# Audio tower on one core: gathers laid out by token quarter, head and slot, an 8-column weight matrix, and a third dense head

## The reference, cut to what matters

```python
kv_scores, indices = _pk(x, Wq_pk, pk_keys)     # per token and head: the 16 best of 4096 rows, with softmax weights
k = jnp.einsum('bnhk,bnhkd->bnhd', kv_scores, keys_table[ind])
v = jnp.einsum('bnhk,bnhkd->bnhd', kv_scores, values_table[ind])
sim = jnp.einsum('bihd,bjhd->bhij', q, k)       # then causal softmax, times v, times Wo
```

## Time and profile before

| | |
|---|---|
| median of 3 runs | 6525.63 us (6495.56 to 6534.32) |
| span of the profiled execution, first to last instruction | 4037.6 us |
| what lies around the span (median less span) | 2488.0 us |
| instructions in the trace | 71484 |
| mean granted clock of TensorE | 0.933 |
| PE, DVE, ACT, POOL busy | 88%, 72%, 68%, 73% of the span |
| indirect DMAs, size | 3072, 201.5 MB |

### The profile page before, as it was taken

How to read it: one execution, slowest core, us unless ns; L and a number is a source line. 1 busy time by engine, 2 the same in 40 slices (tenths; PEclk the granted TensorE clock), 3 DMA queues, 4 the chain that set the end, 5 groups by cost and what they waited for, 6 DMA issues and landing times.

```text
span 4037.6 us, 71484 instructions
## 1 busy us (share of the span) xinstructions
PE 3556.1 (88%) x21240; PEld 2640.5 (65%) x21240; DVE 2916.6 (72%) x13918; ACT 2746.8 (68%) x7870; POOL 2942.1 (73%) x3079
## 2 busy tenths in 40 slices
PE   9789999999989888889888889888889888889677
PEld 6367666667666666667666666666667666667556
DVE  3577778887777777777777777777777777777661
ACT  4467777777767677767677767677767677767444
POOL 0477777777777777777777777777777777777776
PEclk9699999999999999999999999999999999999788
DMA  3112222222222222222222222222222222222211
GB/s 115 30 51 53 54 54 54 53 54 55 54 53 54 54 53 55 54 54 54 55 53 54 54 54 54 54 53 54 54 54 54 54 53 54 54 54 54 53 53 50
DMA packets 108453, 220.17 MB, mean 55 GB/s; under 512 B 55768, under 2 KB 56192, under 8 KB 107552
## 3 DMA queue, kind: packets, MB, share of 16 engines
q0 software_dynamic: 98304, 201.52, 19.0%
q1 hardware_dynamic: 9760, 14.08, 1.1%
HBM read 214.36 MB, written 1.05 MB: 53 GB/s over the span
## 4 chain that ended last, share of the span: by engine, by line
POOL 37%; PE 21%; DVE 15%; issue 15%; ACT 11%; DMA 1%; DVEq 0%; SPq 0%; POOLq 0%; ACTq 0%
POOL got L755 37%; PE bank L1062 5%; ACT diag L1307 3%; PE bank L843 2%; DVE pick L1736 2%; DVE dist L1740 2%; PE bank L1039 2%; PE bank L826 1%; ACT L1093 1%; PE bank L1017 1%; PE bank L829 1%; ACT d_exp L1286 1%; DMA got<-in_table,rows 1%; DVE d_w L1774 1%; DVE rowf L1670 1%
## 5 line engine op out<-in xcount | busy, mean ns | idle before, releaser
L755 POOL DMA_INDIRECT got<-in_table,rows x3072 | 2940.9, 957 | 1085.5 <-issue 925.3
L1307 ACT ACTIVATE diag<-cst,weight 128x128 f32<-128x128 f32 x3072 | 944.7, 393 | 1.0 <-PE bank L1062 0.4
L1062 PE MATMUL bank<-diag,got 128*128 128x128 f32 x6144 | 803.0, 294 | 17.1 <-DMA got<-in_table,rows 9.3
L1062 PEld LDWEIGHTS bank<-diag,got 128*128 128x128 f32 x6144 | 770.3, 207 | 41.5 <-issue 19.5
L1039 PE MATMUL bank<-d_w,tab 128*128 128x128 f32 x4096 | 646.3, 283 | 0.5 <-DVE d_w L1774 0.5
L1774 DVE SCALAR_TENSOR_TENSOR d_w<-bank,d_exp 128x256 f32<-128x256 f32 x1024 | 420.7, 421 | 259.8 <-ACT d_exp L1286 109.3
L1039 PEld LDWEIGHTS bank<-d_w,tab 128*128 128x128 f32 x4096 | 553.8, 196 | 13.2 <-issue 0.8
L1286 ACT ACTIVATE d_exp<-bank 128x256 f32<-128x256 f32 x1024 | 378.2, 376 | 189.8 <-PE bank L1019 188.9
L1017 PE MATMUL bank<-d_top,sel 128*128 128x512 bf16 x1024 | 400.6, 391 | 116.8 <-DVE d_w L1774 116.5
L843 PE MATMUL bank<-h,conv_w 128*128 128x512 f32 (+2 forms) x1024 | 337.7, 478 | 9.3 <-DVE h L1430 7.1
L1017 PEld LDWEIGHTS bank<-d_top,sel 128*128 128x128 bf16 x1024 | 115.5, 113 | 267.0 <-DVE d_w L1774 167.8
(11 more groups left out here) (307 smaller groups left out, 6400.6 us busy)
## 6 DMA issues: line engine op xcount, KB each, us to landing
got<-in_table,rows POOLq DMA_INDIRECT x3072, 2.5
tab<-in_table SPq DMA_DIRECT2D x2, 2048.0 KB, 16.7
got<-in_pairs SPq DMA_DIRECT2D x1, 2048.0 KB, 8.8
wave<-in_x SPq DMA_DIRECT2D x32, 50.0 KB
cst<-in_consts SPq DMA_DIRECT2D x1, 1059.0 KB, 6.9
mlp<-in_mw SPq DMA_DIRECT2D x1, 1024.0 KB, 9.4
out_h<-res_o SPq DMA_DIRECT2D x32, 32.0 KB
conv_w<-in_w SPq DMA_DIRECT2D x1, 512.0 KB, 4.0
```

The source lines that it names most:

```text
L755: pool.indirect_dma_start(got[:, g, k, :], None, table, bass.IndirectOffsetOnAxis(ap=rows[:, h * TOPK + k:h * TOPK + k + 1], axis=0)).then ...
L1062: last = mm(kvt_ps, got[:, j % NGB, k, :], diag[:, j % NDG, k, :], start=k == 0, stop=k == TOPK - 1)
L1307: last = a(diag[:, (b * NG + h) % NDG, k, :], const("ident"), ACT.Copy, scale=weight[:, b % 2, h, k:k + 1])
```

## The change

- Four heads are gathered in pairs, head 4 alone, and heads 5, 6 and 7 are dense. Row numbers and weights are turned by VectorE in 32 x 32 blocks, so that a gather of 128 rows is 4 tokens (one of each quarter) times 2 heads times 16 slots; head 4 is gathered as two halves of the quarter. There are 5 groups of 16 gathers per batch in place of 6.
- A gathered block is multiplied by a matrix of 8 columns (`spread_w`): each column holds the 16 weights of one token and head. VectorE makes it in one instruction per group. The diagonal matrices and the ScalarE work on them are gone, and so is the adding up of 16 products.
- Dense head 5 gets units of its own: 16 "one" units of two chunks each between the 32 "two" units of heads 6 and 7. In a "one" unit ScalarE makes a penalty out of the list distance, TensorE adds it to the scores by a product with `unlisted`, and ScalarE's exponential writes the weights directly; VectorE has no part in it. `UNITS` is 48.
- `rows` gets two buffers, `kvt` one per gathered head, `got` has three in place of four. The dense stage, the sums and the heads become stages of their own in a new table of due times.

```diff
-DENSE = (6, 7)
+DENSE = (5, 6, 7)
...
-UNITS = CHUNKS
+SPLIT = [part for w in range(CHUNKS // 2) for part in (("two", 2 * w), ("two", 2 * w + 1), ("one", 2 * w))]
+UNITS = len(SPLIT)
...
-NGB = 4
+NGB = 3
+SLOTS = 8
...
-        rows = sb("rows", [P, HEADS * TOPK], U32)
...
+        rows = sb("rows", [P, 2, NG * TOPK], U32)
...
+                        if n >= NGB and k % QUARTER == 0:
+                            pool.wait_ge(s_summed, (n - NGB) * (TOPK // QUARTER) + k // QUARTER + 1)
+                        pool.indirect_dma_start(got[:, n % NGB, k, :], None, table,
...
+                    if SOFT[u]:
+                        last = mm(ps[:, 1, at], sel[:, c, :], d_top[:, 1, of, :].rearrange("k i t -> k (i t)"), start=first, stop=end)
...
+                        for i, (c, at) in enumerate(lists):
+                            for k, part in enumerate((d_top[:, 0, of, :], d_mid[:, of, :], d_low[:, of, :])):
+                                mm(pair_bank[u % 2][:, at], sel[:, c, :], part.rearrange("k i t -> k (i t)"), start=i == k == 0, stop=False)
+                        mm(pair_bank[u % 2][:, 0:2 * P], unlisted[:, :], d_pen[:, SOFT_UP_TO[u] % 2, :], start=False, stop=True).then_inc(s_d_out, 1)
...
-                    mm(acc_bank[:, 0:ND * P], const("neg_iota", 0, 1).broadcast_to([P, P]), cst[:, 0:ND * P], start=True, stop=False)
...
+                    last = mm(kvt_ps[:, k * SLOTS:(k + 1) * SLOTS], got[:, n % NGB, k, :], spread_w[:, n % NGB, k, :], start=True, stop=True)
...
-                        last = mm(kvt_ps, got[:, j % NGB, k, :], diag[:, j % NDG, k, :], start=k == 0, stop=k == TOPK - 1)
...
+                        a(d_pen[:, SOFT_UP_TO[u] % 2, :], pair_bank[u % 2][:, 2 * P:4 * P], ACT.Relu, bias=eps[:, 3:4]).then_inc(s_d_pen, 1)
...
+                        a(d_w[:, u % 2, :, :].rearrange("p k t -> p (k t)"), scores, ACT.Exp).then_inc(s_d_soft, 1)
...
-                        last = a(diag[:, (b * NG + h) % NDG, k, :], const("ident"), ACT.Copy, scale=weight[:, b % 2, h, k:k + 1])
...
-                if not isinstance(b, int) or b > 0:
-                    for h in range(first, end):
-                        vec.wait_ge(s_got[((b - 1) * NG + h) % NGB], (((b - 1) * NG + h) // NGB + 1) * 16 * TOPK)
...
+                tt(rows[:, b % 2, a:z], turned[:, a:z], const("row_base", a, z), ALU.add).then_inc(s_rows, 1)
...
+                tt(spread_w[:, n % NGB, :, :].rearrange("p j (q o) -> p j q o", q=4), share, slots, ALU.mult).then_inc(s_spread, 1)
```

More of the change, by code:

```diff
@@ L42 @@
 CHUNKS = NKEY * NKEY // P
-UNITS = CHUNKS
+SPLIT = [part for w in range(CHUNKS // 2) for part in (("two", 2 * w), ("two", 2 * w + 1), ("one", 2 * w))]
+UNITS = len(SPLIT)
+SOFT = [kind == "one" for kind, _ in SPLIT]
+SOFT_UP_TO = [sum(SOFT[:u + 1]) for u in range(UNITS)]
+HARD_UP_TO = [u + 1 - n for u, n in enumerate(SOFT_UP_TO)]
 LORA = 64
@@ L656, in in_turn @@
-        def in_turn(count, late, unit, first, last):
-            def both(prev, cur):
-                if prev is not None:
-                    for u in range(count - late, count):
-                        yield from unit(prev, u)
-                    yield from last(prev)
-                if cur is not None:
-                    yield from first(cur)
-                    for u in range(count - late):
-                        yield from unit(cur, u)
-            return both
+        HOPS = (names(T_HOPS), names(MIX_HOPS), names(ROUTE_HOPS), names(SECOND_HOPS), names(DENSE_HOPS),
+                names([x for g in range(NG) for x in sum_hops(g)]), names([x for p in range(HEADS) for x in head_hops(p)]))
@@ L669, in nothing, with each, program @@
+        def each(count, unit):
+            def program(b):
+                for u in range(count):
+                    yield from unit(b, u)
+            return program
         def nothing(*_):
             return iter(())
-        qpk = diag[0:32, 0, 0:8, :].rearrange("p k d -> p (k d)")
-        pkk = diag[0:32, 0, 8:16, :].rearrange("p k d -> p (k d)")
+        qpk = got[0:32, 2, 0:8, :].rearrange("p k d -> p (k d)")
+        pkk = got[0:32, 2, 8:16, :].rearrange("p k d -> p (k d)")
         LOADS_0 = [(cst[:, 0:CONST_FIRST], consts[:, 0:CONST_FIRST]), (chan[:, :], cvec)]
@@ L1041, in table_sum @@
-                last.then_inc(s_d_sum, 1)
+                listed(b, u)
+                if u == 0 and b > 0:
+                    pe.wait_ge(s_kvd, b)
+                kind, c = SPLIT[u]
+                for i in range(2):
+                    of, chunk = (1 + i, c) if kind == "two" else (0, c + i)
+                    last = mm(acc_bank[:, of * P:(of + 1) * P], tab[:, of, chunk, :], d_w[:, u % 2, i, :],
+                              start=u == i == 0, stop=u == UNITS - 1 and i == 1)
+                last.then_inc(s_d_sum, 1)
@@ L1083, in head @@
                 mm(y_ps, prob_t[:, :], vw[:, :], start=True, stop=True).then_inc(s_y, 1)
-            pipeline(pe, tokenizer, mixer, nothing, dense, nothing, in_turn(HEADS, SCORES_LATE, head, nothing, nothing))
+            pipeline(pe, tokenizer, mixer, nothing, nothing, dense, each(NG, group), each(HEADS, head))
         @block.scalar
@@ L1326, in head @@
                 a(prob_t[:, :], prob_ps, ACT.Copy).then_inc(s_prob_t, 1)
-            pipeline(act, tokenizer, mixer, second, dense, in_turn(NG, SUMS_LATE, weighted, nothing, nothing),
-                     in_turn(HEADS, SCORES_LATE, head, nothing, nothing))
+            pipeline(act, tokenizer, mixer, route, second, dense, each(NG, group), each(HEADS, head))
         @block.vector
@@ L1675, in choose @@
                     yield f"l{k}"
[L1676 removed]
+                    for i in range(of):
                         for r0 in (0, 4):
@@ L1802, in head @@
                 stt(res_o[:, :] if p == HEADS - 1 else res[:, b % 2, :], y_ps, erec[:, :], res[:, b % 2, :], ALU.mult, ALU.add).then_inc(s_added, 1)
[L1804 to L1809 removed]
+            pipeline(vec, tokenizer, mixer, route, second, dense, each(NG, group), each(HEADS, head))
 _OUT = (BATCH, C, D)
```

467 lines of the change are left out of this document (244 added, 223 removed), and 158 rows, old and new, of tables (AT, ENDS_AT).

## The result

The changed kernel took **7348.09 us** (median of 4, 7327.61 to 7358.18) beside 6529.98 us of the kernel before (6495.56 to 6536.48): 1.124 times as long, 95% interval 1.1195 to 1.1287. Slower was right; 7348 lies outside the range of 6240 to 7060.

A forecast was written before the change was run, and what follows sets the result against it. GpSimd's gathers bound the kernel, TensorE close behind; then TensorE: 105.9 + 14.1 + 8.5 - 2.0 = 126.5 us per batch against 119, +240 us, ends +15, so 6525.6 + 255 = 6780 us (+3.9%), range 6240 to 7060.

The forecast's parts named there:

- The starting point, 119 us: Present batch period, set by GpSimd's gathers: 96 gathers at 1.24 us each take 119 us.
- TensorE's added work, +14.1: On TensorE, 16 new "one" units less 16 fewer gathered blocks and smaller items: net +14.1 us per batch (12.2 to 19.1).
- the fall behind L826: Half clock on TensorE after its wait at L826, said to go with that wait: -2.0 us per batch.
- The clock, +8.5: Five gathered groups of 8-column products per batch each cost TensorE one 3.4 us stretch at half clock: 8.5 us.
- the upper bound of 17: Clock price per batch if each group costs two half-clock stretches, or the next group itself runs at 1.2 GHz.
- Idle time, taken as cancelled: TensorE's other 8 idle us per batch, of which some stay, taken to cancel against modelled tails of 0.16 us per gap.
- The wait for landed gathers: VectorE's wait at L1569 before writing new row numbers, 4.8 us per batch, said to go because `rows` has two buffers.
- The ends, +15: The end of the run gets some 15 us longer, since the last batch's 48 units stand alone.
- I take this remainder as unchanged: The 2488 us between the profiled span and the median time, assumed to stay the same after the change.
- both upper prices: Rival, chance 0.12: clock and bf16 products both at their upper price, 140 us per batch, 7210 us.
- TensorE packs perfectly: Rival, chance 0.25: TensorE has no idle time and no group costs clock, period 111 us, 6285 us, faster.
- no clock loss: Rival, chance 0.15: groups on TensorE cost no clock, otherwise as forecast, 118 us per batch, 6510 us, same time.

The follow-up runs named there:

- changed, windows: Changed kernel with block k multiplied by weight columns of blocks k to 15, 68 on average, sums kept: 4185.49 us without stalls, 7188.80 with.

## Why the prediction was wrong

A period is here the time from the first group of batch 8 to that of batch 24, by 16, in traces without stalls:

| us per batch | period | TensorE busy | idle |
|---|---|---|---|
| before | 121.0 | 106.9 | 14.1 |
| changed | 147.6 | 142.5 | 5.1 |
| changed, 128 columns | 125.9 | 120.3 | 5.6 |
| changed, windows | 123.5 | 117.9 | 5.6 |
| before, 8 columns | 133.8 | 131.1 | 2.7 |

- **The starting point, 119 us: too low by 2.** The period of before is 121.0. The prediction took 1.24 us for a gather; their starts are 1.25 apart in the median but 1.263 in the mean, and 96 x 1.263 = 121.2. Its own figure of 1.264 had said so.
- **TensorE's added work, +14.1: right.** At the usual clock (128 columns) it is 120.3 - 106.9 = +13.4, beside 14.1 - 2.0 = 12.1, since the fall behind L826 is in it (half clock for 423 us instead of 519, 1.5 us per batch). Of its parts, the 16 blocks kept their pace: at full clock a group takes 3.5 to 3.7 us to the next instruction with 8, 68 or 128 columns alike, so the columns don't set it. The bf16 products of 128 columns start 0.055 us apart, the lower bound; I had taken 0.07. The Trainium skill ("TensorE: Matmul & The Clock Gate", section on the back-to-back issue gap) has about 81 ns; this trace doesn't agree.
- **The clock, +8.5: the step that failed.** It measured 147.6 - 125.9 = **+21.7**. The step was "if each group costs one stretch of 3.4 us at half clock", with "the units between the groups are dense enough to bring the clock back". The mechanism was right, the size wasn't: a group brings 11.6 us of half clock, of which 2.6 were there anyway (420 us in 160 groups), so 9.0 more, half of it lost, 4.5 x 5 = 22 us. Nor did the units between the groups bring the clock back in time: 81 of the 160 groups ran at half clock from end to end. Even the upper bound of 17 was too low, because it counted a fall or a slow group; here one group makes the clock fall, and the next one, which runs inside the fall, holds it down. The earlier trace rows gave the price of a slow group, and I didn't ask what the slow group does to the clock behind it.
- **Idle time, taken as cancelled: wrong by 5.** 5.1 to 5.6 us are left beside work that fills TensorE. The stop at L826 is gone as said: its successor L743 has 12.8 us of idle time ahead of it in the whole run without stalls, where L826 had 129.8.
- **The wait for landed gathers** is gone, VectorE's 97 us are 925.11 / 1200 x 125.9 = 97.1, ScalarE's 67 are 72. GpSimd stands waiting for L999, as said, but without stalls only 214 us in all; it waits far longer (1396 us) for VectorE's row numbers at L1527, and the prediction did not have this wait.
- **The ends, +15: wrong in sign.** Before 4035 - 32 x 121.0 = 163 us, after 4862 - 32 x 147.6 = 139: -24.
- **The sum.** Period +26.7 instead of +7.5 (the clock 13.2 more, idle time 5.1, starting point and busy time the rest), ends -24 instead of +15: +830 by these, +820 measured, +255 predicted.
- **"I take this remainder as unchanged": the second step that failed.** The 2488 us are not around the span, they are stalls inside it, and the profile of before came from an execution that had none. As a number it came out unchanged, 7348 - 4859 = 2489. That is chance rather than a rule: for the version with windows it is 7189 - 4185 = 3004, for the kernel before with 8 columns 6743 - 4484 = 2259, and spacing the gathers takes nearly all of it away. So the share of time that the stalls hold was the largest thing there was to gain, and the prediction had put it out of sight. The sign was there to be questioned: a page whose span is 38% below every time beside it describes another sort of execution.

Of the rivals, "both upper prices" (7210 us, 0.12) was nearest. Of its two causes the clock was right, and larger than it had it (21.7 us against 17); the bf16 products came out at their lower price, not the upper. "TensorE packs perfectly" fell with the first look at the clock, and "no clock loss" is the version with windows: 118 us of busy time, as it said, but a period of 123.5.

## What to carry to other kernels

Where products take the same time with few columns as with many (here 3.5 to 3.7 us for a group with 8, 68 and 128), narrowing the moving operand saves nothing and can cost the clock: keep the columns, even as columns that are overwritten. Before a profile is read, its span belongs beside the times: if they differ by more than a few us, the profile is not of the executions that are to be explained. And when signals come late in bursts of gathers, try spacing the gathers: it took 34% off this kernel with stalls, and by the sum above it would cost time without them.

## What the runs showed of the hardware

- Back-to-back f32 products of 8 columns, TensorE busy without a pause, brought the clock from 2.4 to 1.2 GHz, 60 times in one run; in the version with 68 columns on average, at the same number of products, no fall came behind a group (mean clock 0.957 against 0.81).
- A group of 16 f32 blocks (32 pairs of weight load and matmul) took 3.5 to 3.7 us at full clock with 8, 68 and 128 columns. Six bf16 products of 128 columns, each with its own weight load, started 0.055 us apart.
- In some series, and not in others on the same chip, TensorE's signals came up to 49 us late while indirect DMAs were issued 1.25 us apart, with pauses from some 7 us after the beginning of a burst on. With bursts of 4 and 8 gathers the latest came 4.5 us late and none was seen in the time; with 1.6 us between gathers none came over 3 us late. ScalarE's signals came within 10 ns in the same trace of the changed kernel. The gathers themselves kept their 1.25 us all the while.
